# Weights and first stage in one program, the second pass's weights in pieces, and other slots for a step's work

## What is computed

```python
attention = jnp.matmul(theta_x, phi_x) / n
out = jnp.matmul(attention, g_x)...            # then conv1x1 w_rec, batch norm, + x
def _mamba(u, ...):
    x, z = jnp.split(u @ in_w.T, 2, axis=-1)
    x = silu(conv_b + sum(xpad[:, k:k + L, :] * conv_w[:, k] for k in range(4)))
    xdbl = x @ xp_w.T
    dt = softplus(xdbl[..., :16] @ dt_w.T + dt_b)
    dA = exp(dt[..., None] * A)                 # A = -exp(A_log), 512 x 16
    dBx = (dt * x)[..., None] * Bm[:, :, None, :]
    # h = dA * h + dBx over the tokens; y = sum over the 16 states of h * C
    y = (y + x * D) * silu(z)
    return y @ out_w.T
x1 = x.reshape(b * h, w, c); x2 = x.reshape(b * w, h, c)
out = einsum('oc,bchw->bohw', cat_conv_w, cat([y1, y2], 1)) + cat_conv_b[...] + x
```

## Time and profile before

| | us |
|---|---|
| median of 3 runs | 6061.89 |
| lowest, highest | 6054.81, 6066.19 |
| the profiled execution | 6065.44 |
| its span, first to last instruction | 6063.2 |
| TensorE busy in it | 5156.5 (85%) |
| VectorE busy | 5064.5 (84%) |
| GpSimd busy | 5070.2 (84%) |
| ScalarE busy | 3544.2 (58%) |
| mean granted clock of TensorE | 0.88 |

### The profile page before, as it was taken

How to read it: one execution, slowest core, us unless ns; L and a number is a source line. 1 busy time by engine, 2 the same in 40 slices (tenths; PEclk the granted TensorE clock), 3 DMA queues, 4 the chain that set the end, 5 groups by cost and what they waited for, 6 DMA issues and landing times. The chain is left out here.

```text
span 6063.2 us, 71214 instructions
## 1 busy us (share of the span) xinstructions
PE 5156.5 (85%) x26046; PEld 3743.4 (62%) x26046; DVE 5064.5 (84%) x3469; ACT 3544.2 (58%) x5534; POOL 5070.2 (84%) x2582
## 2 busy tenths in 40 slices
PE   6968888888888888888868888898889898989887
PEld 5846565666566566566545566566666666666664
DVE  3459899898989898998959989888888888888882
ACT  0056666666666666666636666666666666666662
POOL 0069999999989899999949999898989898888892
PEclk9989898888989897988879988898989898989888
DMA  4132323132322323131321322223232323232323
GB/s 152 70 112 91 102 64 107 62 104 65 102 77 89 98 71 104 63 107 62 104 71 61 102 83 83 97 94 115 88 120 84 118 85 117 86 116 89 113 84 115
DMA packets 242209, 564.60 MB, mean 93 GB/s; under 512 B 29154, under 2 KB 116066, under 8 KB 240324
## 3 DMA queue, kind: packets, MB, share of 16 engines
q1 hardware_dynamic: 231492, 542.49, 27.1%
q10 hardware_dynamic: 10368, 17.57, 0.8%
HBM read 499.84 MB, written 60.13 MB: 92 GB/s over the span
## 5 line engine op out<-in xcount | busy, mean ns | idle before, releaser
L959 POOL TENSOR_TENSOR dbx<-dtx,b_all 128x896 f32<-128x896 f32 x1792 | 3705.0, 2098 | 152.7 <-DVE mamba_ps L903 149.9
L784 ACT ACTIVATE mamba_ps<-dt,w 128x448 f32<-128x448 f32 x3584 | 2131.7, 629 | 1250.6 <-DVE hc L910 1058.3
L903 DVE TENSOR_TENSOR_SCAN mamba_ps<-mamba_ps,dbx 128x896 f32<-128x896 f32 x1232 | 2486.0, 2018 | 419.6 <-ACT mamba_ps L784 335.6
L732 PEld LDWEIGHTS mamba_ps<-ident,hc 128*112 128x112 f32 x14336 | 1837.8, 148 | 647.4 <-issue 385.1
L732 PE MATMUL mamba_ps<-ident,hc 128*112 128x128 f32 x14336 | 2084.8, 300 | 169.0 <-POOL hc L966 89.2
L910 DVE TENSOR_TENSOR hc<-mamba_ps,c_all 128x896 f32<-128x896 f32 x1232 | 1341.5, 1089 | 137.3 <-DVE mamba_ps L903 3.4
L966 POOL TENSOR_TENSOR hc<-hc,c_all 128x896 f32<-128x896 f32 x560 | 1171.8, 2092 | 296.2 <-DVE hc L903 293.5
L903 DVE TENSOR_TENSOR_SCAN hc<-mamba_ps,dbx 128x896 f32<-128x896 f32 x560 | 1128.0, 2014 | 106.9 <-ACT mamba_ps L784 106.9
L637 PE MATMUL mamba_ps<-u,w 128*128 128x448 f32 x1792 | 820.1, 584 | 190.3 <-DVE sz L892 111.3
L646 PE MATMUL mamba_ps<-x,taps 128*128 128x448 f32 (+3 forms) x1792 | 698.4, 533 | 0.2
L637 PEld LDWEIGHTS mamba_ps<-u,w 128*128 128x128 f32 x1792 | 331.2, 203 | 427.7 <-issue 260.8
(11 more groups left out here) (105 smaller groups left out, 3056.2 us busy)
## 6 DMA issues: line engine op xcount, KB each, us to landing
b_all<-bc_scratch SPq DMA_DIRECT2D x448, 448.0 KB, 5.9
c_all<-bc_scratch SPq DMA_DIRECT2D x448, 448.0 KB, 5.7
u<-u_scratch SPq DMA_DIRECT2D x56, 448.0 KB, 3.3
y_scratch<-ytok SPq DMA_DIRECT2D x56, 448.0 KB, 3.3
src<-y_scratch SPq DMA_DIRECT2D x80, 224.0 KB, 4.1
xb<-in_x SPq DMA_DIRECT2D x4, 3136.0 KB, 11.9
u_scratch<-ub ACTq DMA_DIRECT2D x28, 448.0 KB, 8.1
src<-in_x SPq DMA_DIRECT2D x40, 224.0 KB, 4.9
```

Of the source, the lines that this page charges most:

```text
L732: ins = nc.tensor.matmul(y_ps[j % 2][:, c * 128:(c + 1) * 128], hc[g][:, e * T + c * TCH:e * T + (c + 1) * TCH], ident[:, :], start=False, ...
L784: ins = nc.scalar.activation(decay[g % 2][:, e * T:(e + 1) * T], blk(dt[t % 2], j), ACT.Exp, scale=w[:, c:c + 1])
L903: nc.vector.tensor_tensor_scan(dst, h, dbx[n % BX_RING][:, :], 0.0, ALU.mult, ALU.add).then_inc(scan_done, 1)
L959: nc.gpsimd.tensor_tensor(view(dbx[n % BX_RING], 0, [[T, 2], [1, T]]), view(dtx, j * T, [[0, 2], [1, T]]), view(b_all, 2 * g * T, [[T, 2], ...
```

## The change

`prepare` and `attention` become one program, `prologue`. SyncE loads ident and the few weights that the first stage needs, then the small vectors, then the raw weights of pass 1; ScalarE's queue loads x of batches 0, 1 and 2 into three buffers from the start. TensorE turns the eight weight matrices of pass 1 one by one between the pairs 5 to 12 of batch 0, cat's two in batch 1, those of pass 2 in batch 2. The small matrices of a batch (make_r, make_k) are no longer made between its halves but within the next batch's first half or the previous batch's second half, kp, kb and ub being doubled: first_half(0), first_half(1), second_half(0, 1), first_half(2), and so on. The pack of pass 1 is made directly in w, which now lives through both programs, so `mambas` begins without a load of w; the pack of pass 2 alone goes to DRAM.

In `mambas` the two passes are joined. Front items of tile 28 are done in step 27, like those of any other tile, and the BACK items of tile 27 in step 28. w is overwritten in pieces, each when its last reader has passed: x_proj's, dt's and the x half of in_proj behind softplus in step 26 (issued by ScalarE), the z half in step 27, out_proj in step 28 (by SyncE), while A of pass 2 has a buffer of its own, a_next. VectorE makes the new taps in slots 0 to 3 of step 27, and the new skip in its slot 31. dtr moves to other rows of one tile with bc_rows; that changes no shape.

The tables change, and both lags:

```diff
 SCHEDULE = {
-    "z0": (0, 1), "z1": (1, 2), "x0": (2, 3), "x1": (3, 4), ...
-    "c1": (8, 9), ... "out0": (13, 14), "out1": (15, 15),
+    "z0": (0, 0), "x0": (0, 0), "x1": (0, 2), "z1": (0, 3), ...
+    ... "y0": (13, None), "out0": (15, 17), "xp": (16, 19),
...
-SILU_Z_AT, SILU_X_AT, SOFTPLUS_AT = 8, 16, 24
-TAKE_Y_AT = {4: 3, 12: 0, 20: 1, 28: 2}
-GATE_AT = {7: 3, 16: 0, 24: 1, 31: 2}
+SILU_Z_AT, SILU_X_AT, SOFTPLUS_AT = 9, 16, 25
+TAKE_Y_AT = {5: 3, 13: 0, 22: 1, 28: 2}
+GATE_AT = {8: 3, 15: 0, 25: 1, 29: 2}
...
-POOL_LAG, SUMS_LAG = 4, 3
+POOL_LAG, SUMS_LAG = 3, 4
```

The order of TensorE's work in the prologue, and the weights of the second pass:

```diff
+                for n in EARLY:
+                    turn(n)
+                pe.wait_ge(copied, len(EARLY))
+                first_half(0)
+                first_half(1)
+                second_half(0, 1)
+                first_half(2)
+                second_half(1, 2)
+                first_half(3)
+                second_half(2, 3)
+                second_half(3, None)
...
-                        upto(sp, y_stored, 16 * t)
-                        sp.dma_start(w[:, :], w_dram[t // TILES]).then_inc(w_ready, 16)
+                        sp.dma_start(a_next[:, :], w_dram[:, W_A:W_A + DB * NST]).then_inc(a_loaded, 16)
                         spread_bc(t)
+                    if t == CHANGE - 1:
+                        sp.wait_ge(work_ready, Item(t, "z3").ready())
+                        sp.dma_start(halves(w, DIN), halves(w_dram, DIN)).then_inc(z_loaded, 16)
...
+                    if t == CHANGE:
+                        sp.wait_ge(work_ready, Item(t - 1, "out1").ready())
+                        sp.dma_start(w[:, W_OUT:W_OUT + DB * FEAT], w_dram[:, W_OUT:W_OUT + DB * FEAT]).then_inc(out_loaded, 16)
...
+                def load_front():
+                    it = Item(CHANGE - 1, "dt3")
+                    act.wait_ge(work_free[it.slot], it.freed())
+                    act.dma_start(halves(w, 0), halves(w_dram, 0)).then_inc(front_loaded, 16)
+                    act.dma_start(w[:, W_XP:W_A], w_dram[:, W_XP:W_A]).then_inc(front_loaded, 16)
...
+                        if t == CHANGE - 1 and n < DB:
+                            if n == 0:
+                                dve.wait_ge(front_loaded, 32)
+                                dve.wait_ge(work_ready, Item(t, "c3").ready())
+                            make_taps(n)
+                        if t == CHANGE - 1 and n == SLOTS - 1:
+                            dve.wait_ge(sums_done, SLOTS * t + 3 * GP + 1)
+                            make_skip()
```

More of the change, by code:

```diff
@@ new lines, in turn @@
+                def turn(n):
+                    srcs, rows, cols, _ = jobs[n]
+                    if n == EARLY[0]:
+                        pe.wait_ge(small_in, 16 * len(smalls))
+                    if n == M0[0]:
+                        pe.wait_ge(raw_ready[0], 16 * 6)
+                    if n == CAT[0]:
+                        pe.wait_ge(cat_in, 16)
+                    if n == M1[0]:
+                        pe.wait_ge(raw_ready[1], 16 * 6)
+                    if n not in EARLY:
+                        pe.wait_ge(copied, n)
+                    for r, s in enumerate(srcs):
+                        o = job_bank(n) * 512 + r * cols
+                        p = s.shape[0]
+                        last = nc.tensor.transpose(ps[0:rows, o:o + cols], s, ident[0:p, 0:p])
+                    last.then_inc(turned, 1)
@@ new lines, in project @@
+                def project(b, i):
+                    upto(pe, pg_taken, PAIRS * b + i - 1)
+                    for h in range(2):
+                        n0 = (2 * i + h) * HALF
+                        for k in range(2):
+                            last = nc.tensor.matmul(bank(i % 2)[0:HALF, h * 256:(h + 1) * 256],
+                                                    xb[b % 3][:, k * NPOS + n0:k * NPOS + n0 + HALF],
+                                                    wpg[:, k * 256:(k + 1) * 256], start=(k == 0), stop=(k == 1))
+                    last.then_inc(pg_ready, 1)
@@ new lines, in add_pair @@
+                def add_pair(b, i):
+                    pe.wait_ge(pg_taken, PAIRS * b + i + 1)
+                    if i == 0:
+                        upto(pe, k_dve, 4 * (b - 1) + 1)
+                    for h in range(2):
+                        s = pg[i % 2]
+                        last = nc.tensor.matmul(bank(2)[:, 0:CMID], s[0:HALF, h * 256 + 128:h * 256 + 256],
+                                                s[0:HALF, h * 256:h * 256 + 128],
+                                                start=(i == 0 and h == 0), stop=(i == PAIRS - 1 and h == 1))
+                    last.then_inc(mt_step, 1)
@@ new lines, in first_half @@
+                def first_half(b):
+                    pe.wait_ge(x_ready[b % 3], 16 * (b // 3 + 1))
+                    for i in range(PAIRS):
+                        project(b, i)
+                        if i:
+                            add_pair(b, i - 1)
+                        if b == 1 and i == 1:
+                            make_r(0)
+                        if b == 1 and i == 4:
+                            make_k(0)
+                        for n in WITH_PAIR.get((b, i), ()):
+                            turn(n)
+                    add_pair(b, PAIRS - 1)
@@ new lines, in second_half @@
+                        last.then_inc(ut_ready, 1)
+                        if then is not None and i == 1:
+                            make_r(then)
+                        if then is not None and i == 4:
+                            make_k(then)
+                for n in EARLY:
+                    turn(n)
+                pe.wait_ge(copied, len(EARLY))
[4 more added lines that the diff above has]
+                second_half(1, 2)
@@ new lines, in _ @@
+                for m in range(2):
+                    last = nc.vector.memset(pack[m][:, W_DT:W_DT + DIN], 0.0)
+                last.then_inc(cleared, 1)
+                dve.wait_ge(small_in, 16 * len(smalls))
+                for n in EARLY:
+                    take_turn(n)
+                dve.wait_ge(vectors_in, 16 * len(vectors))
+                gamma, var, beta, mean, brec = (bn[:, i * W2:(i + 1) * W2] for i in range(5))
+                nc.vector.tensor_scalar_add(var, var, BN_EPS).then_inc(chain, 1)
@@ L472, in mambas @@
         ytok = sb("ytok", 4 * FEAT, TCH)
[L473 to L474 removed]
+        rows = sb("rows", T, 2 * NST + 32)
+        bc_rows = rows[0:2 * NST, :]
         restart = sb("restart", 4 * TSEQ)
```

614 lines of the change are left out of this document (303 added, 311 removed), and 8 rows, old and new, of the table SCHEDULE.

## The result

The changed kernel takes 5616.26 us (median of 4 runs, 5609.5 to 5617.14); the kernel before, run beside it, 6060.89 us. The ratio is 0.9264, 95% interval 0.9248 to 0.928: 7.4% faster. The profiled execution has a span of 5615.2 us. The forecast was 5650 us, with 5560 to 5800 as its range: the sign and the size were right, and most of the places; four terms of the sum were not (the slack kept in the ordinary steps, the start of the prologue, the change of weights and the end), and their errors partly cancel.

A forecast was written before the change was run, and what follows sets the result against it. VectorE and GpSimd were taken to set a 90.7 us floor per step, with ScalarE's lateness causing the waits above it. First scan 316.3, first step 94, steps 3230.5, +4, late steps 1805, end 202 gave about 5650 us; range 5560 to 5800.

The forecast's parts named there:

- (1): Slots in the steps: later takes of out_proj's results bring ordinary steps to 92.3 us, 1.6 above the 90.7 floor.
- rival A: Steps near the floor, ScalarE and TensorE never late: 91.0 us ordinary, 92.3 late, 5555 us in all; chance 0.22.
- (2): GpSimd weighs one dbx sooner in the steps: cost 0, gain 2 us for those awaiting slot 26's weighing.
- (3): Late steps, with part of the last convolution: earlier fetch and regrouped pieces give 95.0 us, bounds 92.3 and 99.
- (4): Prologue: the first stage starts at 24 us, lasts 237 us and ends at 261.
- (5): First stage's end to first scan: w's load and the wait for taps go; scan at 316.3 us, before 367.7.
- (6): Change of weights: 164.0 us become a 92.3 us step plus 4.1 us of small products, 96.4; bounds 92.3 and 110.
- the rule on the shared interface: At the weight change, VectorE's small products may collide with GpSimd on SBUF: at most 4.1 us once more.
- (7): End of the run: one more group of sums to drain, +1 us, and the last step, +1 us.
- B: TensorE takes over, its clock low after new standing places: steps 94.8 and 99 us, 5815 us; chance 0.25.
- C: Waits only move: steps stay at 97.7 and 101.1, only prologue and transition are won, 5951 us; chance 0.06.
- D: Slower steps, GpSimd's weighing waiting close behind the scan: 104.7 us a step, 6269 us; chance 0.02.

The follow-up runs named there:

- e8: Changed kernel with one more of a step's 32 weighings on GpSimd (slot 12; 11 instead of 10): 5677.13 us.
- e5: Changed kernel, but ScalarE takes out_proj's two results in the slots where TensorE makes them (15 and 18, not 17 and 20): 6021.27 us.
- e7: Changed kernel with TensorE's sums three slots behind instead of four (SUMS_LAG 3, POOL_LAG still 3): 5618.48 us.
- e6: Changed kernel with GpSimd's weighing four products behind the scan instead of three (POOL_LAG 4): 5622.64 us.
- e2: Changed kernel with tap and skip matrices made on VectorE by a product of two tensors instead of tensor and per-partition scalar: 5618.72 us.
- e10: Kernel before, with the new slot table, new slots of silu, softplus, gates and takes, and new lags; old prologue and weight change: 5714.48 us.
- e4: Changed kernel with the old slot table, old slots of silu, softplus, gates and takes, and old lags: 5965.7 us.

## Why the forecast was right, and where it wasn't

**What bounds the kernel.** Right. The floor of 90.7 us, read from the two engines' waits, is what the steps now last. e8 shows that GpSimd stands at it, and VectorE's waits of 0.6 us a step say the same of VectorE.

**(1) Slots.** The mechanism was right: without the room for out_proj's results (e5) all of the gain in the steps is gone. The size was off: of the 1.6 us that I kept above the floor 0.1 came, so the ordinary steps are rival A's. Over 34 steps that is 51 us, the largest miss. The reason for keeping them was that TensorE would stand for silu_x and at slot 30. It does stand, 2.03 us at x_proj where I said 3, and 123.7 us in 26 steps, 4.8 a step, for in_proj's banks where I said 5. But VectorE doesn't wait for it: the sums can come late by that much without stopping VectorE, and with SUMS_LAG 3 they still can (e7). The misfit that I had worked out for silu_x, 0.1 us, is 0.24 in the trace.

**(2) POOL_LAG.** Cost 0 is right (e6). The gain of 2 us for those who wait for slot 26's weighing isn't: taking it back moved the fetch by 1.4 us and the late step by 0.4.

**(3) Late steps.** 95.0 forecast, 95.2 measured, from two errors that cancel. The 92.3 it stands on was 90.8, and the stall left was 4.4 us instead of 2.7. Fetch to TensorE was 6.5 us (6.3 in the sum), and TensorE to the take of fb1 7.6 us, where I had taken 1 us off 7.3. The group of sums is gone from between the pieces, but the clock stays low for longer: before, the first 8 products took 3.33 us and the next 4 and 8 took 1.01 and 1.68; now they take 3.33, 1.70 and 2.22. The first term, 2.1 us for the weighing, is the one that failed most: behind the scan of slot 26 (means of 18 steps) the fetch stood 5.1 us before and stands 4.7 now, and the last product ended 19.3 us behind it and ends 18.7.

**(4) Prologue.** The start was forecast at 24 and came at 29.9. The term that failed is the landing of the constants, forecast near 14 us, measured at 21.75: the issues took 4 us more than 0.5 us each, and the last load took 7.6 us to land instead of 4.1. The root took 0.9 us instead of 1.7, the chain 7.3 as said. (The sum as written, 14 + 1.7 + 7.3, is 23 and not 24; and 242.4 - 14.4 + 8 is 236 and not 237.) The stage lasted 233 us instead of 237. **(5)** From its end (262.9) to the scan 57.3 us instead of 55.3: 10.8 to the load of u, 3.6 for it instead of 4.5, and 42.9 instead of 40.6 from there. Together 320.2 instead of 316.3.

**(6) Change of weights.** Mechanism named, size wrong: 20 small products were to cost 4.1 us, at most twice that by the rule on the shared interface. They cost 21.2 us: 112.0 against 90.8, and with the products on ScalarE 91.7. The rule as I had cited it names no price; that it would cost the product at most its own length once more was my reading. It is a wait for the length of the other engine's instruction: half of the 20 took about 2.1 us instead of 0.28 (one of them 1.2), and the others fell into gaps of GpSimd. The Trainium skill, SBUF — State Buffer, Who interferes with whom, states it so: whoever comes first has the shared ports for its whole instruction and the other blocks; and it counts a product of two SBUF tensors in, as e2 shows. The upper bound of 110 didn't hold either: with all 20 held up it would have had to be 134 (92.3 + 20 x 2.1).

**(7) The end.** +2 forecast, -6 measured. It came with the table: from the last scan to the end are 107.3 us here, 107.0 in e10, and 115.5 in e4 with the old one (113.2 in the kernel before). SUMS_LAG has no part in it (107.4 in e7). Which entry does it stays open.

**The total.** It is nearer to the measurement than its terms are, and part of that is luck: ordinary steps, first step and end were forecast 61 us too long, prologue, change of weights and late steps 23 us too short.

**The rivals.** A came true in the ordinary steps, not in the late ones. B's mechanism is there, in the late steps of the changed kernel and in e5, but not each new place where TensorE stands lowered its clock: where it waited 2.03 us ahead of x_proj the granted clock stayed at 1.00. The mean clock in the steps rose from 0.87 to 0.93; with two levels, 1.00 and 0.50, that is an estimate of 14% of the time at the low one instead of 26%, and VectorE hardly waits for it. C and D are out: steps fell by 6.7 us, and GpSimd's waits went from 7.0 to 0.4 us.

## What to carry to other kernels

Ask of each wait how much work stands between the maker and the taker in each engine's list: two results taken two slots after they are made were the condition for 351 us, while the lags between VectorE, GpSimd and TensorE had slack and gave nothing. Before putting a small VectorE instruction with all operands in SBUF beside a busy GpSimd, price it at one GpSimd instruction each (here 2.1 us for 9 of 20, in e2 once 4.2), or give it to ScalarE. A load that TensorE waits for costs twice when the wait lets its clock fall: here the wait, and up to 2.6 us of slow products behind it.

## What the runs showed of the hardware

- A 128 x 128 product of VectorE with all operands in SBUF took 0.26 to 0.28 us while GpSimd stood and about 2.1 us while it was inside an instruction of 2.06 to 2.17 us, once 4.2; ScalarE's took 0.39 us beside the same GpSimd.
- Eight products of TensorE took 1.69 us at a granted clock of 1.00 and 3.33 us after 5.45 us of idleness, with 0.50 behind it. After 2.03 us of idleness the clock stayed at 1.00.
- The first two issues of the bn loads took SyncE's queue 3.54 us together, with a load of 3136 KB and eight smaller ones under way.
